# A second mixture of experts computed by dispatch, with four-value register loads and finer waits, in a two-layer perceiver kernel

## What is computed

```python
# layer 0, E = 64 experts, TOP_K = 8, hidden width 96
logits = x @ gate_w.T
scores = softmax(logits); topk_w, topk_ids = top_k(scores, 8)
topk_w = topk_w / (topk_w.sum(-1) + 1e-20)
y = sum over the 8 chosen e of topk_w * (silu(x @ w_gate[e]) * (x @ w_up[e])) @ w_down[e]

# layer 1, E = 8 experts, TOPK = 2, hidden width 512
h = _layernorm(x, ln2_g, ln2_b).reshape(B * S, D)
logits = h @ gate_w + gate_b
topv, topi = top_k(logits, 2); gw = softmax(topv)
hid = relu(einsum('td,edf->etf', h, W1) + b1)
out_e = einsum('etf,efd->etd', hid, W2) + b2
moe = einsum('etd,te->td', out_e, ew)      # ew: gw at the two chosen experts, 0 elsewhere
return x + moe
```

## Time and profile before

| | us |
|---|---|
| median of three runs | 3863.2 |
| profiled execution, its own time | 3865.37 |
| its span | 3863.6 |
| granted TensorE clock, mean over the span | 0.909 |
| PE busy | 3139.7 (81%) |
| DVE busy | 2202.4 (57%) |
| ACT busy | 1664.8 (43%) |
| POOL busy | 1411.5 (37%) |

### The profile page before, as it was taken

How to read it: one execution, slowest core, us unless ns; L and a number is a source line. 1 busy time by engine, 2 the same in 40 slices (tenths; PEclk the granted TensorE clock), 3 DMA queues, 4 the chain that set the end, 5 groups by cost and what they waited for, 6 DMA issues and landing times. The chain is left out here.

```text
span 3863.6 us, 90063 instructions
## 1 busy us (share of the span) xinstructions
PE 3139.7 (81%) x30574; PEld 2540.3 (66%) x30574; DVE 2202.4 (57%) x5866; ACT 1664.8 (43%) x4673; POOL 1411.5 (37%) x2430
## 2 busy tenths in 40 slices
PE   7999999997742006998799999999987777569998
PEld 5666666666642005887677777777765656459998
DVE  4777676766567303665677776667755556641111
ACT  4666666664520002333244444444435556434443
POOL 1222222222237771000777777777632222220000
PEclk9999999998975558999899999999998998769999
DMA  2000000000021413555111111111100000000000
GB/s 78 22 16 22 18 20 22 16 17 2 0 122 50 131 55 112 150 152 146 35 34 33 33 33 33 33 33 33 30 6 2 0 2 0 1 11 12 11 11 22
DMA packets 158242, 150.49 MB, mean 39 GB/s; under 512 B 18680, under 2 KB 137728, under 8 KB 157696
## 3 DMA queue, kind: packets, MB, share of 16 engines
q1 hardware_dynamic: 141696, 114.86, 9.8%
q0 software_dynamic: 16384, 33.59, 2.9%
HBM read 95.95 MB, written 52.43 MB: 38 GB/s over the span
## 5 line engine op out<-in xcount | busy, mean ns | idle before, releaser
L1656 POOL DMA_INDIRECT y_picked<-f_ys,idy x256 | 246.9, 965 | 394.7 <-POOLq L92 352.5
L1523 ACT ACTIVATE y_prob<-y_ps_s,y_mx 128x514 f32<-128x514 f32 x256 | 176.5, 690 | 445.2 <-DVE y_mx L1731 445.2
L2276 POOL DMA_INDIRECT f_xs<-acc,f_idx x256 | 255.8, 999 | 102.3 <-issue 83.3
L1336 PEld LDWEIGHTS y_ps_o<-y_v,y_pT 128*128 128x128 f32 x2048 | 248.8, 191 | 59.7 <-issue 42.0
L1336 PE MATMUL y_ps_o<-y_v,y_pT 128*128 128x64 f32 x2048 | 272.0, 276 | 11.0 <-DVE y_om L1824 9.7
L77 POOL TENSOR_TENSOR x_px<-x_prob,consts 128x64 f32<-128x64 f32 x256 | 75.9, 296 | 560.2 <-ACT x_prob L856 560.2
L2681 ACT ACTIVATE g_hid<-g_ps_h,g_b 128x512 f32<-128x512 f32 x256 | 176.1, 688 | 240.5 <-PE g_ps_h L100 237.8
L856 ACT ACTIVATE x_prob<-x_ps_s,x_mx 128x289 f32<-128x289 f32 x512 | 250.8, 496 | 45.9 <-DVE x_mx L1017 42.3
L2697 DVE SCALAR_TENSOR_TENSOR x<-g_ps_y,g_w_now,x 128x128 f32<-128x128 f32 x256 | 72.1, 344 | 345.5 <-PE g_ps_y L2647 345.5
L1024 DVE COPY x_pT<-x_ps_t 128x512 f32<-128x512 f32 x256 | 177.1, 692 | 144.3 <-PE x_ps_t L644 140.3
L2472 PE MATMUL fe_ps_x<-consts,fe_xg 128*128 128x128 f32 x384 | 75.5, 278 | 208.7 <-DMA fe_xg<-f_xs 208.6
(11 more groups left out here) (443 smaller groups left out, 8779.3 us busy)
## 6 DMA issues: line engine op xcount, KB each, us to landing
fe_xg<-f_xs SPq DMA_DIRECT2D x192, 128.0 KB, 2.1
f_ys<-fe_yk SPq DMA_DIRECT2D x192, 128.0 KB, 2.1
x_ctxT<-ctx_dram SPq DMA_DIRECT2D x32, 514.0 KB, 3.5
y_ctxT<-ctx_dram SPq DMA_DIRECT2D x32, 514.0 KB, 3.6
f_weights<-w_one_dram SPq DMA_DIRECT2D x1, 10240.0 KB, 28.1
f_xs<-f_zeros SPq DMA_DIRECT2D x64, 128.0 KB, 1.8
f_xs<-acc,f_idx POOLq DMA_INDIRECT x256, 2.2
y_picked<-f_ys,idy POOLq DMA_INDIRECT x256, 2.5
```

Source lines behind the costliest of these rows:

```text
L1336: mm = pe.matmul(ps_o[:, b, at:at + GW], pT[:, u % 2, g, c, :], v[:, b % 2, c, g * D + at:g * D + at + GW], start=(u == 0 and g == 0 and c ...
L1523: ins = act.activation(prob[:, p, :, :], ps_s[:, 2 * p:2 * p + 2, 0:M], ACT.Exp, bias=mx[:, p:p + 1], accum_out=den[:, s, b, p:p + 1])
L1656: pool.indirect_dma_start(out=picked[:, t % 2, k * D:(k + 1) * D], out_offset=None, in_=ys, in_offset=bass.IndirectOffsetOnAxis(ap=idy[:, ...
L2276: pool.indirect_dma_start(out=xs, out_offset=bass.IndirectOffsetOnAxis(ap=idx[:, t, k:k + 1], axis=0), in_=acc[:, t, :], in_offset=None).t ...
```

## The change

Four things are changed together.

1. **Second mixture by dispatch.** `route` is gone. `route_one` is generalized to `dispatch`, called for both mixtures. For the second it has 8 columns and 2 choices per token: POOL scatters 64 times, SP writes 8 tails, and one memset and one wait are new in each group. The layer norm's gain and bias are applied where ACT copies the transposed rows, in the routing and again in the expert block. All weights (w1, w2 and biases spread over the partitions, 6.5 MB) are loaded by four DMAs issued before the routing and waited for in the expert block. There, 72 blocks of 128 rows are worked off; a third block gathers the two rows of each token with 64 indirect DMAs on POOL, adds them with two DVE operations per tile, and stores the output in 8 pieces of 4 tiles as they get ready. The last block of `perceiver` is gone. The three-part products are gone from this mixture: it multiplies float32 directly.
2. **Blocks of 128 in the first mixture.** 192 blocks of 256 rows become 320 of 128, worked off in 160 pairs with one expert number for each half. A pair takes two loads of 64 KB. The stores are issued by ACT instead of SP, and SP's loads run up to eight pairs ahead.
3. **Four-at-a-time register loads.** `load_four` reads four neighbouring table entries with one call: on SP and PE once for two pairs in the first mixture, and on SP, PE and DVE once for four blocks in the second. On PE it stands between up(j+2) and turn_h(j+1) in the first mixture, and behind down(j) in the second.
4. **Per-batch waits.** `keys_a` waits for the split of its own batch instead of for all four.

The diff, cut to its core:

```diff
+def load_four(nc, eng, row, at, top):
+    return nc.values_load_multi_w_load_instructions(row[:, at:at + 4], engines=(eng,), min_val=0, max_val=top)[1]
...
             def keys_a(t, s, j):
-                if j == 0:
-                    pe.wait_ge(S["ctx_split"].sem, S["ctx_split"].upto(t))
+                pe.wait_ge(S["ctx_split"].sem, S["ctx_split"].upto(t, j + 1))
...
-REGION = B * N + 2 * P
-BLOCK = 2 * P
-BLOCKS = 192
+REGION = B * N + P
+BLOCK = P
+BLOCKS, BLOCKS2 = 320, 72
+PAIRS = BLOCKS // 2
...
-def route_one(nc, sh, d, xs, idx, idy, w8, tab):
+def dispatch(nc, sh, prefix, E, TOP, BLOCKS, src, normed, xs, idx, idy, share, tab):
...
+                if not first:
+                    dve.memset(top[:, :, TOP:8], LOWEST).then_inc(S["cut"].sem, 1)
+                    dve.wait_ge(S["cut"].sem, S["cut"].upto(i))
...
                 def load(j):
...
-                    at = sp.value_load(tab[0:1, 0, j:j + 1], min_val=0, max_val=E1 * REGION - BLOCK)
-                    sp.dma_start(xg[:, s, :, :], xs[bass.ds(at, BLOCK), :].rearrange("(c p) d -> p c d", p=P))\
-                        .then_inc(x_in[s].sem, 16)
...
+                    if j % 2 == 0:
+                        at[j], at[j + 1] = (lambda v: (v[0:2], v[2:4]))(
+                            load_four(nc, mybir.EngineType.SP, tab[0:1, 0, :], 2 * j, E1 * REGION - BLOCK))
+                    for c in range(2):
+                        sp.dma_start(xg[:, s, c, :], xs[bass.ds(at[j][c], BLOCK), :]).then_inc(x_in[s].sem, 16)
...
-                for j in range(-3, BLOCKS):
-                    if j + 3 < BLOCKS:
+                for j in range(-3, PAIRS):
+                    if j + 3 < PAIRS:
                         turn_x(j + 3)
-                    if 0 <= j + 2 < BLOCKS:
+                    if 0 <= j + 2 < PAIRS:
                         up(j + 2)
-                    if 0 <= j + 1 < BLOCKS:
+                    if j + 3 < PAIRS and (j + 3) % 2 == 0:
+                        find(j + 3)
+                    if 0 <= j + 1 < PAIRS:
                         turn_h(j + 1)
...
+                def store(j):
+                    s = j % RING
+                    act.wait_ge(S["y_kept"].sem, S["y_kept"].upto(j))
+                    act.dma_start(ys[j * 2 * BLOCK:(j + 1) * 2 * BLOCK, :].rearrange("(c p) d -> p c d", p=P),
+                                  yk[:, s, :, :]).then_inc(y_out[s].sem, 16)
...
+        dispatch(nc, sh, "g", E2, TOP2, BLOCKS2, acc, rows, xs, idx, idy, share, tab)
...
+            @block.tensor
+            def _(pe):
...
+                    pe.transpose(ps_x[:, b, 0:P], xg[:, s, :], ident).then_inc(S["xT_turned"].sem, 1)
...
+                    pe.matmul(ps_u[:, b, :], xT[:, b, :], w1[:, bass.ds(expert[j // 4][j % 4], 1), :], start=True, stop=True)\
+                        .then_inc(S["up_made"].sem, 1)
...
+                    for k in range(K):
+                        mm = pe.transpose(ps_h[:, b, k * P:(k + 1) * P], up_s[:, b, k, :], ident)
...
+                    for k in range(K):
+                        mm = pe.matmul(ps_y[:, b, 0:D], hid[:, b, k, :], w2[:, bass.ds(expert[j // 4][j % 4], 1), k, :],
+                                       start=k == 0, stop=k == K - 1)
...
+                for j in range(-3, BLOCKS2):
+                    if j + 3 < BLOCKS2:
+                        turn_x(j + 3)
+                    if 0 <= j + 2 < BLOCKS2:
+                        up(j + 2)
+                    if 0 <= j + 1 < BLOCKS2:
+                        turn_h(j + 1)
+                    if j >= 0:
+                        down(j)
+                    if j + 3 < BLOCKS2 and (j + 3) % 4 == 0:
+                        find(j + 3)
...
+                    act.activation(xT[:, b, :], ps_x[:, b, 0:P], ACT.Identity, bias=cols[:, b_:b_ + 1],
+                                   scale=cols[:, g:g + 1]).then_inc(S["xT"].sem, 1)
...
+                    act.activation(hid[:, b, :, :], ps_h[:, b, :].rearrange("p (k n) -> p k n", k=K), ACT.Relu)\
+                        .then_inc(S["hid"].sem, 1)
...
+                pool.tensor_tensor(acc[:, :, :], acc[:, :, :], x[:, :, :], ALU.add)
...
+                    dve.tensor_tensor(up_s[:, b, :, :].rearrange("p k n -> p (k n)").unsqueeze(1),
+                                      ps_u[:, b, :].unsqueeze(1), b1[:, bass.ds(expert[j // 4][j % 4], 1), :], ALU.add)\
+                        .then_inc(S["up_kept"].sem, 1)
...
+                        pool.indirect_dma_start(out=picked[:, s, k, :], out_offset=None, in_=ys,
+                                                in_offset=bass.IndirectOffsetOnAxis(ap=idy[:, t, k:k + 1], axis=0))\
+                            .then_inc(rows_in[s].sem, 16)
...
+                for n in range(TILES // RUN):
+                    sp.wait_ge(S["added"].sem, S["added"].upto((n + 1) * RUN - 1))
+                    sp.dma_start(table[:, n * RUN:(n + 1) * RUN, :], acc[:, n * RUN:(n + 1) * RUN, :])\
+                        .then_inc(stored.sem, 16)
```

More of the change, by code:

```diff
@@ L40 @@
 CONSTS = {"ident": 128, "same8": 128, "head8": 16, "head16": 8, "head8s": 16, "head16q": 4, "quad": 16, "own4": 4, "own4s": 4,
-          "pick": 32, "batch": 4, "iota": 8, "one": 1, "upper": 128, "region": 64, "starts": 16, "blocks": 192}
+          "pick": 32, "batch": 4, "iota": 8, "one": 1, "upper": 128, "region": 64, "starts": 32, "blocks": 320}
 def const_offset(name):
@@ L2186, in route_one @@
                 "kept total part den inv weighted ranked based val found slots same scaled w8 carry carried "
-                "zeros tails counted cmp blocks first ends started table")
-    zeroed = Signal(nc.alloc_semaphore(name="f_zeroed"), 16)
-    scattered, step = Signal(nc.alloc_semaphore(name="f_scattered"), 16), Signal(nc.alloc_semaphore(name="f_step"))
+                "cut zeros tails counted cmp blocks first ends started table")
+    zeroed = Signal(nc.alloc_semaphore(name=f"{prefix}_zeroed"), 16)
@@ L2464, in _, with find @@
                 expert = {}
+                def find(j):
+                    four = load_four(nc, mybir.EngineType.PE, tab[0:1, 1, :], 2 * j, E1 - 1)
+                    expert[j], expert[j + 1] = four[0:2], four[2:4]
                 def turn_x(j):
@@ L2657, in _ @@
-        @block.gpsimd
-        def _(pool):
-            with pool.Fori(0, E2 // 2) as i:
-                for s in range(2):
-                    e = i * 2 + s
-                    pool.wait_ge(weights[s].sem, weights[s].upto(i))
-                    pool.wait_ge(S["up_made"].sem, S["up_made"].upto(e - 2, U * K))
-                    copy(pool, w1_hi[:, s:s + 1, :], w1[:, s:s + 1, :], sh["one"]).then_inc(S["rounded"].sem, 1)
-                    pool.wait_ge(S["rounded"].sem, S["rounded"].upto(e))
-                    pool.tensor_tensor(w1_lo[:, s, :], w1[:, s, :], w1_hi[:, s, :], ALU.subtract)\
-                        .then_inc(S["split"].sem, 1)
@@ L2669, in _ @@
-        @block.scalar
-        def _(act):
-            act.sem_inc(S["hidden"].sem, K)
-            with act.Fori(0, E2 // 2) as i:
-                for n, (s, c) in enumerate(units):
-                    e = i * 2 + s
-                    for k in range(K):
-                        if k == 0:
-                            act.wait_ge(S["down_made"].sem, S["down_made"].upto(e, c - 1))
-                            if c == 0:
-                                act.wait_ge(weights[s].sem, weights[s].upto(i))
-                        act.wait_ge(S["up_made"].sem, S["up_made"].upto(e, c * K + k + 1))
-                        act.activation(hid[:, n % 2, k, :], ps_h[:, k, :], ACT.Relu, bias=b1[:, s, k:k + 1])\
-                            .then_inc(S["hidden"].sem, 1)
@@ L2774, in perceiver @@
         if "e" in phases:
-            experts_two(nc, sh, d)
-        with nc.Block() as block:
-            @block.sync
-            def _(sp):
-                res = sh["acc"] if "m" in phases and "e" not in phases else x
-                sp.dma_start(out.rearrange("(t p) d -> p t d", p=P), res[:, :, :]).then_inc(stored, 16)
-                sp.wait_ge(stored, 16)
+            experts_two(nc, sh, d, out)
 def _swap(w):
```

507 lines of the change are left out of this document (208 added, 299 removed).

## The result

The changed kernel takes **3686.3 us** (median of 4 runs, 3684.1 to 3689.4) against 3865.2 (3858.0 to 3872.2) for the kernel before on the same chip: ratio **0.954**, 95% interval 0.952 to 0.956. Its profiled run took 3685.5 us, with a span of 3683.7. The forecast was 3703.

A forecast was written before the change was run, and what follows sets the result against it. It took SP, with PE close behind, to bound the first experts, and PE, running all eight experts, the second mixture. 3863.6 - 129 (second mixture) - 31 (first experts) - 0 (cross attention) = 3704 us span, 3703 against the median; range 3640 to 3775.

The forecast's parts named there:

- 0.18 us per block for the exposed load: Second experts: PE's four-value load, once in four blocks, leaves 0.7 us exposed, 0.18 per block on top of 2.30.
- 0.8 us of cover: Second experts: 0.8 us of PE's 1.4 us four-value load is covered, leaving 0.7 exposed with 0.1 to get going.
- 1.9 per pair: First experts: PE needs 1.54 us plus half of the exposed 0.7, 1.89; 160 pairs take 304 us instead of 335.
- the 1.4 us of one load with four checks: PE's four-value load: one load instruction of 0.30 us and four times about 0.28 for the rest make 1.4 us.
- PE's sequencer is 0.7 to 0.8 us ahead of its array: First experts, kernel before: this lead narrowly hides PE's single register load, whose load, check and assert take 0.6 us.
- SP at about 1.75: First experts: SP's two loads with address work take 1.03 us per pair, half a four-value load 0.7: about 1.75.
- PE now decides: First experts: PE at 1.89 us per pair sets the pace; SP's slack of 0.15 takes in its occasional slow issue.
- The load's time doesn't grow with its values: Register loads: the rival said it does grow, 4 x 0.30 us, 2.3 with checks, kernel 3791 us; dear loads' chance 0.18.
- The cheap load: Rival: four values cost 0.6 us, nothing exposed, kernel 3634 us, or 3666 if only SP pays; cheap loads' chance 0.17.
- Cross attention two: nothing: The finer split wait gains 0 us because PE then waits for y_ka_sin; rival of 30 us gained, 3673, chance 0.09.
- 23 us per group of DVE: Second routing: DVE takes 23 us per group against 20.3 for POOL's 16 scatters, so DVE sets the pace.
- The serial chain: Rival, second experts: a block's engine steps don't overlap, 6 us per block, 432 in all, kernel 3956 us; chance 0.04.

The follow-up runs named there:

- e4: Changed kernel with PE's four-value load in the first mixture moved behind down(j): 3714.3 us, ratio 0.9620 to the kernel before.
- e11: Changed kernel, first mixture: PE loads two values with checks every pair instead of four every second, SP without checks: 3761.1 us, ratio 0.9733 to the kernel before.
- e2: Changed kernel with PE's four-value loads without their range checks: 3678.4 us, ratio 0.9534 to the kernel before.
- e5: Changed kernel with four single-value loads on PE, each with its check, in place of one load of four: 3789.6 us, ratio 0.9805 to the kernel before.
- e3: Changed kernel with the four-value loads on every engine without range checks: 3625.8 us, ratio 0.9389 to the kernel before.
- e7: Changed kernel with DVE's sum in cross attention two cut to two of its eight rows: 3655.9 us, ratio 0.9463 to the kernel before.
- e8: Changed kernel with DVE's sum cut to two of eight rows and PE waiting for all four splits again: 3675.0 us, ratio 0.9516 to the kernel before.
- e6: Kernel before, with the first expert stage's stores issued by ACT and SP's loads up to eight steps ahead: 3841.0 us, ratio 0.9938 to the kernel before.
- e12: Changed kernel, first mixture: PE loads two values every pair, neither PE nor SP with range checks: 3655.2 us, ratio 0.9447 to the kernel before.
- e9: Changed kernel with DVE's sum and following addition in cross attention two moved to unit 7 of a tile: 3769.8 us, ratio 0.9753 to the kernel before.

## Why the prediction was right, and where its steps were not

**The size of the gain** came out, 179 us against 160, and the range held it. Of the 19 us over, the second mixture has 24 and the first experts 4, less the 8 of the stages forecast as unchanged.

**Second experts, 15 us.** The term 0.18 us per block for the exposed load was wrong. Blocks follow at 2.30 us, as I had it from PE's rows, and a load hardly shows: 9.26 per four blocks against 9.92 forecast (4 x 2.48). PE's 18 loads of the stage (17 times 9.26 from the first to the last):

```profile
L55 PEldq TENSOR_LOAD <-g_tab x18: 327/332/334, 3422.6 to 3580.1; - x18
```

That is 12 us of the 15; filling and draining take the other 3 less. I had carried over 0.8 us of cover from the first mixture. But in the second the sequencer has 6.0 us of work for 9.2 of matmuls, and in the first 3.5 for 3.1.

**First experts, 4 us.** The forecast of 1.9 per pair (measured 1.87), the 1.4 us of one load with four checks (1.57 to the next instruction) and the 0.7 exposed (0.63) all look right. The step behind them was not: "PE's sequencer is 0.7 to 0.8 us ahead of its array" was read as a cover that a load can use up once and win back. The account that fits the runs is the sum in the table, with 1.0 us per pair for waits and register operations that I had not counted at all. That the cover gave nearly the same number was chance, and it gave e4 and e11 wrongly. SP at about 1.75 was right for a round without slow issues (1.73); with them it is 1.84, and e2 ran into it at that. So "PE now decides" with 0.15 us of slack on SP was too sure, and the sign that SP has idle time didn't come (1.2 us). PE and SP were so near each other that naming one of them as the bound meant little.

**Rivals.** The load's time doesn't grow with its values: 0.33 against 0.30. e5, with four loads in place of one, shows what that rival would have cost. The Trainium skill (Runtime: NRT & Kernel Launch, Instruction fetch mechanics) has about 200 ns per register even in bulk; by its figure, an estimate, four values would take 0.8 us. It says so of loads from HBM, and these are from SBUF. The trace doesn't agree here: 0.33 us on PE and 0.30 on SP. The cheap load (0.6 with checks) was wrong by its checks: 0.28 us each. What that would have given, 3634, is nearly what e3 gives without them, 3625.8.

**Cross attention two: nothing.** Right, and for the reason given, as e7 and e8 show. That not all of PE's wait comes back when the cover is gone, I had not allowed for.

**Second routing.** 110 against 115. 23 us per group of DVE was too much: it took 20.3, just what POOL needs for 16 scatters. So "DVE sets the pace here" wasn't borne out, and the gaps between POOL's groups didn't come. 20 until the first scatter, 80 until the last and 10 to the first load are the whole stage. The gather stage was 5 us shorter than forecast: 2 by its pace (1.25, not 1.27) and 3 by its two ends.

**The serial chain** didn't come: the window of the second experts has PE busy 170 of 176 us.

## What to carry to other kernels

Add up an engine's sequencer like any other resource: its waits and register operations take 0.125 us each from start to start, though the profile shows 0.05, and each range check 0.28 (all on PE); where that sum is over the array's time per step, the array has gaps, and the one other place tried for the load (e4) made the stage 33 us longer. Four neighbouring values in one load cost about as much as one, so batch the load and drop checks that the maker of the table already ensures, on all engines that have them, or the next one takes over. A finer wait pays only if the engine behind it isn't already held by another; look for the row that ends at the next wait.

## What the runs showed of the hardware that I had not expected

- A register load on PE doesn't have one price. In the kernel before, 144 of 192 took 0.30 us on average and 48 took 0.50. At 0.2 us after their start about 4 DMA packets were in flight for the first and 17 for the second, counted over the trace's packets. e4 (0.50, about 14 in flight) goes with that. e3 and e6 don't: in e3 loads of 0.33 had 9 in flight, and in e6 the 37 loads under 0.4 us had 13 and the 155 longer ones 9. So traffic alone doesn't explain it, and the cause stays open.
- Nor does it explain the load of two values: 0.53 at least in all of e11 and e12, with 3 packets in flight in e11 and 6 in e12 on average, where four values take 0.33 and one 0.30 at best. It stands in the same place of the program as the changed kernel's four-value load, only in every pair. Whether the form of the load makes it dear, or its coming twice as often, remains open.
- In e4 the sequencer stood 0.46 to 0.60 us at a wait that had been met in time before, and issued nothing meanwhile. So moving a load can turn a harmless wait into a stall.
- In e9 the granted clock fell for 3.4 us or more behind 28 of the 29 gaps of about 2 us in PE's work. PE's busy time rose by 42 us, more than the 32 us of the longer gaps themselves. Behind the gaps of 0.9 us for the same key product, in the changed kernel, it didn't fall.
